# The low parts of 26 weight pieces: the second 512 columns of each moved from VectorE to GpSimd in two operations

## What is computed

```python
x = L0_attn_x                                   # (8, 512, 256)
x = x + attention(layernorm(x))                 # 16 heads of 16, causal softmax, W_qkv, W_out
xn = layernorm(x)                               # and again inside the expert layer, with gamma, beta
probs = softmax(xn @ gate_w)                    # 8 experts
w, idx = top_k(probs, 2);  w = w / sum(w)
h = gelu(xn @ w1[e] + b1[e])                    # w1: (8, 256, 1024)
out_e = h @ w2[e] + b2[e]                       # w2: (8, 1024, 256)
x = x + sum(w * out_e over the two experts) + residual
```

## Time and profile before

| what | value |
|---|---|
| time, median of 3 runs | 992.68 us (991.67 to 997.17) |
| profiled execution, its span | 991.0 us |
| PE busy | 872.7 us, 88% |
| DVE busy | 722.9 us, 73% |
| ACT busy | 587.6 us, 59% |
| POOL busy | 461.7 us, 47% |

### The profile page before, as it was taken

One profiled execution on the slowest core, in us unless ns is written; L12 is line 12 of the kernel. 1 busy time (PEld: TensorE's weight loads), 2 busy tenths in 40 slices (PEclk: granted clock), 3 DMA queues, 4 the chain that ended last, 5 costly groups with the idle time before them and its releaser, 6 DMA issues.

```text
span 991.0 us, 21222 instructions
## 1 busy us (share of the span) xinstructions
PE 872.7 (88%) x6870; PEld 576.0 (58%) x6870; DVE 722.9 (73%) x1658; ACT 587.6 (59%) x1079; POOL 461.7 (47%) x561
## 2 busy tenths in 40 slices
PE   4999988787788888897878898989989999999996
PEld 3655422242433434352424686879869989989875
DVE  6578878758578797969893785885766766666664
ACT  2776566656678686858776562554544455445453
POOL 2000123334425747655667546574476464544441
PEclk9999977876887978677987997999989999999998
DMA  9988667654857676575727452242223232323231
GB/s 213 293 275 256 207 180 220 177 139 120 215 168 225 172 189 183 159 191 150 201 77 232 125 120 39 46 85 51 47 36 54 50 49 46 56 50 50 36 52 19
DMA packets 146327, 130.09 MB, mean 131 GB/s; under 512 B 59344, under 2 KB 128848, under 8 KB 146096
## 3 DMA queue, kind: packets, MB, share of 16 engines
q1 hardware_dynamic: 115648, 87.51, 31.8%
q0 software_dynamic: 15680, 18.95, 12.0%
q10 hardware_dynamic: 14896, 22.28, 7.1%
HBM read 83.63 MB, written 44.80 MB: 130 GB/s over the span
## 4 chain that ended last, share of the span: by engine, by line
PE 49%; DVE 17%; issue 10%; DMA 9%; POOL 6%; SPq 5%; ACT 3%; POOLq 1%; ACTq 0%; another core or an unknown queue 0%; DVEq 0%
PE banks L769 15%; PE banks L787 14%; PE banks L582 4%; PE banks L697 3%; PE banks L685 3%; DVE arena L1230 3%; PE banks L641 2%; PE banks L572 2%; DVE weights L1384 2%; DMA weighed_values<-arena 2%; POOL out L1702 2%; DVE arena L1232 2%; POOL slot_tokens L1649 2%; PE banks L626 2%; DMA inverse_sums<-arena 2%
## 5 line engine op out<-in xcount | busy, mean ns | idle before, releaser
L991 ACT ACTIVATE arena<-banks,arena 128x256 f32<-128x256 f32 (+1 forms) x312 | 152.2, 541 | 192.9 <-issue 126.8
L769 PE MATMUL banks<-arena,weights 128*128 128x256 f16 (+1 forms) x1872 | 207.4, 266 | 11.5 <-issue 8.6
L787 PE MATMUL banks<-weights,arena 128*128 x1704 | 197.5, 275 | 3.6 <-DVE arena L1514 2.6
L769 PEld LDWEIGHTS banks<-arena,weights 128*128 x1872 | 174.0, 98 | 39.5 <-issue 16.2
L1702 POOL DMA_INDIRECT out<-arena x71 | 115.6, 1628 | 168.4 <-DVE arena L1525 131.8
L787 PEld LDWEIGHTS banks<-weights,arena 128*128 128x128 f16 x1704 | 166.4, 99 | 26.9 <-issue 6.4
L641 PE MATMUL banks<-arena 50*128 50x128 f16 (+3 forms) x512 | 126.4, 352 | 37.9 <-DMA arena<-arena 12.2
L1512 DVE TENSOR_SCALAR arena<-arena 128x512 f16<-128x512 f32 (+1 forms) x156 | 77.1, 494 | 70.6 <-ACT arena L991 58.9
L613 PE MATMUL banks<-arena 48*128 48x384 f16 (+3 forms) x512 | 103.1, 345 | 26.4 <-DVE arena L1233 9.3
L1514 DVE SCALAR_TENSOR_TENSOR arena<-arena 128x512 f16<-128x512 f32 (+1 forms) x156 | 111.0, 711 | 5.6
L641 PEld LDWEIGHTS banks<-arena 50*128 50x128 f16 x512 | 39.1, 102 | 128.7 <-issue 43.3
(11 more groups left out here) (190 smaller groups left out, 1338.9 us busy)
## 6 DMA issues: line engine op xcount, KB each, us to landing
weights<-in_L_ffn_w ACTq DMA_DIRECT2D x16, 1024.0 KB, 7.8
arena<-in_L_ffn_w SPq DMA_DIRECT2D x32, 512.0 KB
qk_parts<-weights SPq DMA_DIRECT2D x64, 128.0 KB
arena<-qk_parts SPq DMA_DIRECT2D x128, 64.0 KB, 3.2
weighed_values<-arena SPq DMA_DIRECT2D x32, 256.0 KB
token_rows<-arena SPq DMA_DIRECT2D x12, 512.0 KB, 4.3
arena<-qk_parts SPq DMA_DIRECT2D x128, 32.0 KB, 3.3
arena<-weighed_values SPq DMA_DIRECT2D x32, 128.0 KB
```

The costliest lines, as they stand in the source:

```text
L769: m = pe.matmul(bank[:, c * TILE:c * TILE + WIDTH[j]], w1[:, k, wp, f:f + P], xp[:, k, 0:WIDTH[j]], start=(i == 0), stop=(i == len(terms) ...
L787: m = pe.matmul(bank[:, c * D:(c + 1) * D], hp[:, f, c * P:(c + 1) * P], w2[:, f // (FC // 2), wp, f % (FC // 2), :], start=(f == 0 and i ...
L991: m = act.activation(h_32[r % 2][:, c, 0:WIDTH[j]], banks[:, 1 + c2, c * TILE:c * TILE + WIDTH[j]], ACT.Gelu, bias=b1_now[j % 2][:, 2 * c2 ...
```

## The change

For the 26 pieces that stay on chip, VectorE's `low_weights` covers the first 512 columns of the piece. A new step `low_rest` on GpSimd, at the same tick, covers the other 512 columns: first raw x scale in place, then minus the high part. Both wait for the high part. Whatever waited for VectorE's low part (the next raw load into the same buffer, the first tile of the experts, the first layout step) now waits for both. The first 6 pieces stay as they were.

```diff
--- before.py
+++ after.py
@@ -357,6 +357,8 @@
             at(base - (30 if i < LENT else 35), "load_raw", i)
             at(base, "high_weights", i)
             at(base + 9, "low_weights", i)
+            if i >= LENT:
+                at(base + 9, "low_rest", i)
             if i < LENT:
                 at(base + 15, "store_weights", i)
 
@@ -756,6 +758,7 @@
                 xh, xl = xt_high[j % 2], xt_low[j % 2]
                 w.wait_ge(sem("xt_low"), j + 1)
                 w.wait_ge(sem("w_low"), W_SPLITS)
+                w.wait_ge(sem("low_rest"), W_SPLITS - LENT)
                 w.wait_ge(sem("late_in0"), 16 * LATE_FIRST)
                 if j > 0:
                     w.wait_ge(sem("gelu"), FC // 2 * (j - 1) + c2 + 1)
@@ -1380,8 +1383,8 @@
                 w.wait_ge(sem("w_high"), i + 1)
                 if 0 < i < LENT:
                     w.wait_ge(sem("w_stored"), 32 * i)
-                high, low = parts_of(i)
-                v.scalar_tensor_tensor(low, w_raw[raw_buffer[i]], SCALE_W[splits[i][1]], high, ALU.mult,
+                high, low = (x[:, 0:HALF if i < LENT else HALF // 2] for x in parts_of(i))
+                v.scalar_tensor_tensor(low, w_raw[raw_buffer[i]][:, 0:low.shape[1]], SCALE_W[splits[i][1]], high, ALU.mult,
                                        ALU.subtract).then_inc(sem("w_low"), 1)
 
             laid_at = [0]
@@ -1650,6 +1654,15 @@
                         slots_dram[:, :], bass.IndirectOffsetOnAxis(slot_index[b % 2][:, tt, k:k + 1], 0),
                         token_of[:, TT * b + tt:TT * b + tt + 1], None).then_inc(sem(f"placed{b % 2}"), 16)
 
+            def low_rest(i):
+
+                w.wait_ge(sem("w_high"), i + 1)
+                raw = w_raw[raw_buffer[i]][:, HALF // 2:HALF]
+                high, low = (x[:, HALF // 2:HALF] for x in parts_of(i))
+                scaled = own.mark(g.tensor_scalar(raw, raw, SCALE_W[splits[i][1]], None, ALU.mult))
+                w.wait_ge(own.sem, scaled)
+                g.tensor_tensor(low, raw, high, ALU.subtract).then_inc(sem("low_rest"), 1)
+
             def mask(u, part):
                 p = p_T[u % 2]
                 if part < 2:
@@ -1724,6 +1737,8 @@
                     w.wait_ge(own.sem, m)
                     g.tensor_tensor(rows, rows, over_tiles(beta), ALU.add).then_inc(
                         sem("beta_added"), 1)
+                elif stage == "low_rest":
+                    low_rest(n)
                 elif stage == "lay_slots":
                     lay_slots(n)
                 elif stage == "gather":
@@ -1830,6 +1845,8 @@
             def load_raw(i, e_, m_, k_):
                 if raw_before[i] is not None:
                     w.wait_ge(sem("w_low"), raw_before[i] + 1)
+                    if raw_before[i] >= LENT:
+                        w.wait_ge(sem("low_rest"), raw_before[i] - LENT + 1)
                 elif i > 0:
                     w.wait_ge(sem("w_stored"), 32 * LENT)
                 n = (KC, FC)[m_]
```

## The result

The changed kernel takes 1007.67 us (median of 4 runs, 1003.69 to 1011.92), the kernel before 992.17 us beside it (4 runs). The ratio is 1.0138, with a 95% interval of 1.0097 to 1.0178: slower by 13.7 us at the 992.68 us of before. On that scale the changed kernel stands at 1.0138 x 992.68 = 1006.4 us (1002.3 to 1010.3). The forecast was 996.0 us with a range of 985 to 1006, so that the result lies right at the upper end, and 4.4 us above the 1002.0 of the rival "GpSimd is the bound". By the prediction's own limit of 0.5% the kernel is slower, to which it had given a chance of 0.38; it had given most, 0.44, to the same.

The account below looks back on a forecast made before the run. VectorE was taken to bound a good part of the 200 us stretch. The terms -7.4 + 0.5 + 2.0 + 3.1 + 1.2 + 1.0 + 3.0 = +3.4 us, with the 992.68 us median, gave 996.0 us, range 985 to 1006.

Parts of the forecast that it names:

- GpSimd is the bound: Second rival, GpSimd in attention: masks' lateness passes in full, 11.5 us; +9.3 us in all, 1002.0 us; chance 0.21.
- the prediction's own limit of 0.5%: Whole kernel: about 5 us counts as no change, 987.7 to 997.6; faster 0.18, same 0.44, slower 0.38.
- the rivals: VectorE's gain comes through, 985.3 us, chance 0.19; GpSimd is the bound, 1002.0, 0.21; collisions decide, 1002.2, 0.12.
- the price of the pair: GpSimd's two new operations per piece: 0.65 + 1.27 = 1.92 us, with starts 2.07; bounds 1.3 and 2.5 us.
- its absorptions: PE's waits of 2.49, 0.48 and 0.38 us and a 4.2 us lead for VectorE take up part of the masks' lateness.
- The gain: VectorE's low parts: each half saves 0.53 us, 14 of 26 on the chain of waits, 7.4 us.
- The late masks: PE's weighing at 340, 394 and 504 us starts 3.0, 4.5, 4.0 us late; 0.5, 2.0, 3.1 us remain.
- The wait goes in the lateness: At 340 us: PE's later 2.49 us wait for VectorE takes up most of 3.0 us of lateness, leaving 0.5 us.
- The threshold: GpSimd's pair: the rival in which GpSimd is the bound decides from about 2.5 us a pair; 2.07 us was taken.
- The late loads: Raw loads wait for GpSimd's half: 1.2 us at 362.52 us, through ScalarE, and 1.0 us allowed elsewhere.
- The collisions: VectorE and GpSimd exclude each other on on-chip reads: 3.0 us; as a rival 9.1 us, 1002.2 us, chance 0.12.

Follow-up runs that it names:

- the run with the two-input scaling: Changed kernel with GpSimd's multiplication written as a two-input operation, the factor read as a 128 x 512 tile with step zero: 1007.58 us, ratio 1.0131 to before.
- the nine pairs in the gaps: Changed kernel with only 9 of 26 pieces shared, those where GpSimd had waited before its next masks; VectorE makes the other 17 whole: 998.11 us, ratio 1.0011.
- the nine in the runs: Changed kernel with only 9 of 26 pieces shared, those in GpSimd's solid runs ahead of the late masks; VectorE makes the rest: 1007.21 us, ratio 1.0123.
- the runs with 1.2 and 2.2 us a piece: Changed kernel without GpSimd's multiplication (1.2 us, 975.75 us, ratio 1.0046), and with four memsets in place of its pair (2.2 us, 976.92 us, ratio 1.0065).
- the four memsets: Changed kernel with GpSimd's pair replaced by four memsets, 2.2 us together, that read nothing on chip: 976.92 us, ratio 1.0065 to before.
- the half alone: Changed kernel without GpSimd's pairs: VectorE makes its 512 columns, GpSimd only writes zeros for the rest long before: 965.37 us, ratio 0.9947 to before.
- five memsets: Changed kernel with GpSimd's pair replaced by five memsets of the same length, reading nothing on chip, raw loads still waiting: 1008.08 us, ratio 1.0128.

## Why the prediction was off, step by step

The direction was right, a net loss through late masks and late loads, but the forecast of +3.4 us (its own sum gives 996.1 us) stands against +13.7. That the range reached the result is owed to the margin for the rivals, "and a little over", not to the forecast's own terms.

**The step that failed** is the price of the pair: "I take 0.65 + 1.27 = 1.92 us a pair". The first operation was sized by a mask instruction, because that one also has one input. It measures 1.57 us, and the pair 2.77 us with its gaps instead of 2.07, above even the upper bound of 2.5. The nearer row was the other arithmetic one, L1640, although it has two inputs. By it the pair would have been 2.54 us, at the point from which the prediction let its second rival decide.

That rival is what happened. With 2.77 us in the prediction's own steps the masks are 4.4, 6.6 and 5.4 us late (an estimate), 16.4 us in place of 11.5, and the rival's sum becomes 16.4 + 2.2 + 3.0 - 7.4 = +14.2 us. The forecast's sum, with its absorptions left in, becomes about +8.3. So by this estimate the price is about half of the miss and the absorption the other half. That the first sum meets the measured 13.7 so closely is in part luck, as its other terms were off in both directions, see below. And the run with the two-input scaling, whose pair of 2.2 us gave no smaller ratio, leaves open how much a cheaper pair would have saved.

**The gain** of 7.4 us measures 5.1 (2.2 to 8.1) when GpSimd is left out of it. The step holds.

**The late masks.** The places at 340, 394 and 504 us were right, and one more, at 452, was missed (0.8 us net). The prediction left 0.5, 2.0 and 3.1 us of lateness there; it grows by 5.4, 6.0 and 5.0, in which the late loads are contained. A part of this is the price. The rest is the absorption: "The wait goes in the lateness". It does go: PE stands 2.5 us less between 340 and 366. But the prediction put at nothing what PE's work costs behind a wait. The same work took 2.3 us more, at a granted clock of 0.64 instead of 0.80, so that 5.2 of 5.4 us were left. Two kernels on one chip show the same: with the nine pairs in the gaps, where PE waits 1.27 us for the mask at this place, the same steps (340.70 to 366.53) take PE 20.5 us at a clock of 0.81; with the nine in the runs, behind 5.40 us, 25.4 us at 0.56 (345.17 to 373.50). No run sets the clock by itself, so this holds for this place as the rows show it, and further on the clock gave time back.

**The threshold** was wrong with it. On one chip the runs with 1.2 and 2.2 us a piece both lose, 1.0046 and 1.0065 against 0.9947 without a pair. At the 2.07 us that the prediction took, the time would have been nearer 999 us (1.0065 x 992.68, an estimate by the four memsets on the faster chip) than 996.

**The late loads**, 2.2 us in the sum, measure 2.7 us by the ratios and 4.8 by the medians, with overlapping intervals. The prediction looked for them at ScalarE, whose waits for raw pieces did grow, from 2.7 to 8.3 us. It did not see the second way, at 406 us, through a small copy for PE that stood in SP's queue behind a raw load. It had named inverses, queries and keys behind such a load, not this copy.

**The collisions**, 3.0 us in the sum. The changed kernel's VectorE is busy for 17 us more than that of the half alone. But five memsets, with 8 us less of it, give the same time, so that at least these 8 us cost nothing that can be told from zero. The rule of the Trainium skill (SBUF — State Buffer, section Who interferes with whom) has its case again in the kernel with five memsets: there the longest half takes 2.74 us and begins at 385.52, 0.17 us after a two-input addition of GpSimd's, L1733, which runs until 387.72. The warning of the Trainium skill (Perfetto Trace Analysis, section Optimizing Scalar/DVE Operations) that offloading between these engines might not help came true here, by 13.7 us. But its reason, the port that the two engines share, is not what decided: the five memsets do not read, and lose as much.

## What to carry to other kernels

Work that is moved to an engine with 63% of a stretch is paid at the place where it is put, not at the engine's mean: nine pairs made the kernel 1.1 us slower where GpSimd had waited (within the error), and 12.3 us in front of its late masks. Size an operation that the trace lacks by the arithmetic of that engine, and run it once by itself before you rest a sum on it. Do not count a wait as a full reserve: look at the granted clock of the work behind it as well, since PE gave 2.5 us of waits here and lost 2.3 us of them to slower work. And when a transfer gets one more engine to wait for, follow everything behind it in its queue.

## What the hardware showed that was not expected

- On GpSimd a multiplication of 128 x 512 float32 numbers in place takes 1.57 us with one input and a factor for each partition, 1.49 us with a constant, and 1.04 us as an operation with two inputs of which the second has a step of zero. At 128 x 256 the one-input form takes 0.92 us: about 0.28 us to start and 1.3 us for 512 columns, by these two.
- A memset of GpSimd's takes 0.525 us for 128 x 512 numbers, whether they are float32 or float16.
- The subtraction that writes float16 takes 1.16 us, the two-input operation that writes float32 1.27 us (L1640 before), and the multiplication of a float32 tile by a broadcast factor 1.04 us.
- After PE had stood for 5.62 us, its granted clock was 0.50 over the next 3.85 us and 0.64 over the next 25.5 us. In the same steps before, without that stand, it was 1.00 over the first 5.1 us and 0.80 over 25.7 us.
- Three chips ran the kernel before at 971.10, 994.39 and 996.09 us. Compare with a run on the same chip, and kernels of two chips, by their ratios, only with care.
